# A two-layer decoder on one core: the first expert layer sorts its token-expert pairs into tiles and multiplies only the chosen ones

## What is computed

```python
TOP_K, NUM_EXPERTS = 4, 16          # H = 256, I = 224
logits = einsum('bsh,eh->bse', x, router_w) + expert_bias
top_w, top_idx = top_k(softmax(logits), TOP_K)
top_w = top_w / sum(top_w)
g = einsum('bsh,khe->bske', x, gate_proj)     # every expert, every token
u = einsum('bsh,khe->bske', x, up_proj)
out = einsum('bske,keh->bskh', silu(g) * u, down_proj)
sel = take_along_axis(out, top_idx)
y = sum(sel * top_w)                          # added to the residual stream
```

## Time and profile before

| | us |
|---|---|
| median of 3 runs | 4774.38 (4768.8 to 4774.94) |
| the profiled execution | 4788.41, of which span 4786.6 |
| set attention: its loads start / its first matmul | 707 / 714 |
| expert layer: router loads start / main loop starts / last addition to `x` ends | 808 / 831 / 1497 |

### The profile page before, as it was taken

The page is one execution under the profiler, slowest core; times in us unless marked ns, Lnnn a source line. Parts: engine busy times, 40 slices in busy tenths (PEclk is TensorE's granted clock), DMA queues, the critical chain, the costliest instruction groups (busy, mean ns, idle before and its releaser), DMA issues. The chain is left out here.

```text
span 4786.6 us, 58979 instructions
## 1 busy us (share of the span) xinstructions
PE 3923.9 (82%) x18543; PEld 2940.0 (61%) x18543; DVE 2799.6 (58%) x7765; ACT 1611.4 (34%) x3960; POOL 1349.6 (28%) x2074
## 2 busy tenths in 40 slices
PE   6999976999997799999999999983999999960230
PEld 4666654555555578888888888872556565640230
DVE  4666654222222788888888888844666666653123
ACT  2444431111111455545455554521444444420000
POOL 0000000000000365455555455540111111116447
PEclk9999986999997999999999999996999999985665
DMA  1000000000000011111111111111000000011240
GB/s 65 0 0 0 0 8 24 12 12 23 12 12 18 20 37 23 41 38 24 36 23 40 35 29 36 24 18 51 1 0 0 0 0 0 0 64 58 60 143 13
DMA packets 198749, 119.39 MB, mean 25 GB/s; under 512 B 122312, under 2 KB 187654, under 8 KB 197520
## 3 DMA queue, kind: packets, MB, share of 16 engines
q1 hardware_dynamic: 181472, 102.85, 8.3%
q0 software_dynamic: 12288, 9.55, 0.7%
q10 hardware_dynamic: 4800, 4.72, 0.3%
HBM read 102.09 MB, written 38.93 MB: 29 GB/s over the span
## 5 line engine op out<-in xcount | busy, mean ns | idle before, releaser
L1630 DVE SCALAR_TENSOR_TENSOR dl_y<-ps,dl_taps,dl_y 128x255 f32<-128x255 f32 (+2 forms) x1536 | 653.0, 474 | 131.4 <-ACT dl_y L1526 127.3
L1361 PE MATMUL ps<-xnT,dl_wkqv 128*128 128x256 f32 x2048 | 543.4, 391 | 33.9 <-DVE dl_lp L1673 26.4
L923 PE MATMUL ps<-xnT,moe_wgu 128*112 x1024 | 447.3, 595 | 5.2 <-DVE moe_ex L963 5.2
L1361 PEld LDWEIGHTS ps<-xnT,dl_wkqv 128*128 128x128 f32 x2048 | 367.9, 193 | 84.0 <-issue 39.2
L923 PEld LDWEIGHTS ps<-xnT,moe_wgu 128*112 128x112 f32 x1024 | 181.9, 178 | 251.3 <-issue 249.3
L362 POOL TENSOR_TENSOR at_rs<-at_ss,mhalf 128x15 f32<-128x15 f32 x32 | 125.5, 3921 | 745.9 <-DVE at_ss L549 745.9
L183 POOL TENSOR_TENSOR ln_rstd<-ln_ve,mhalf 128x4 f32<-128x4 f32 x24 | 24.2, 1010 | 1084.0 <-DVE ln_ve L169 1084.0
L1284 POOL TENSOR_TENSOR dl_rn<-dl_n,mhalf 128x4 f32<-128x4 f32 x128 | 173.7, 1357 | 548.2 <-DVE dl_n L1646 548.2
L448 PE MATMUL ps<-at_shared,at_v 128*128 128x256 f32 (+2 forms) x1280 | 315.9, 380 | 4.6
L989 DVE TENSOR_TENSOR moe_hT<-moe_sg,ps 112x1024 f32<-112x1024 f32 x64 | 78.2, 1221 | 372.6 <-ACT moe_sg L947 372.6
L1526 ACT ACTIVATE dl_y<-ps,dl_taps 128x256 f32<-128x256 f32 x512 | 260.2, 560 | 95.4 <-PE ps L1361 95.4
(11 more groups left out here) (278 smaller groups left out, 8195.3 us busy)
## 6 DMA issues: line engine op xcount, KB each, us to landing
dl_grow<-decay_rows SPq DMA_DIRECT2D x128, 128.0 KB, 3.0
sp_wgu<-in_w1gu SPq DMA_DIRECT2D x12, 768.0 KB, 10.2
dl_wkqv<-in_w1kqv SPq DMA_DIRECT2D x16, 512.0 KB, 4.7
delta_diag<-dl_lp SPq DMA_DIRECT2D x512, 8.0 KB, 1.5
dl_diag<-delta_diag_tt SPq DMA_DIRECT2D x512, 8.0 KB, 1.7
moe_wgu<-in_w0gu SPq DMA_DIRECT2D x16, 448.0 KB, 3.7
slot_rows<-sp_zero SPq DMA_DIRECT2D x4, 1152.0 KB, 8.1
sp_wd<-in_w1d SPq DMA_DIRECT2D x12, 384.0 KB, 11.5
```

The costliest lines, as they stand in the source:

```text
L923: last = nc.tensor.matmul(k.ps[h][0:IC, m, :], wgu[q][h][:, c, m * IC:(m + 1) * IC], k.xnT[:, c, ds(g * (GT * P), GT * P)], start=c == 0, ...
L1361: last = nc.tensor.matmul(bank(h, m // 2, (m % 2) * S, (m % 2 + 1) * S), wkqv[h][:, c, m * P:(m + 1) * P], k.xnT[:, c, u.seq * S:(u.seq + ...
L1630: last = nc.vector.scalar_tensor_tensor(y[h][:, m, back:S], bank(h, m // 2, (m % 2) * S, (m % 2 + 1) * S - back), taps[h][:, m, KC - 1 - b ...
```

## The change

The layer is rewritten as `routed_experts`. What it does, in order:

- All 16 experts' weights are loaded at once into SBUF by a new `ExpertWeights`, 32 transfers (16 of 448 KB and 16 of 224 KB) that SP issues before `set_attention`.
- `layernorm` leaves its rows in `rows`, beside which DVE writes the 16 routing weights of each token. SP stores these 2,048 rows of 272 values in HBM (`xtab`) and `k.x` in HBM (`acc`).
- The pairs are counted and sorted: DVE makes running counts per expert, PE adds them over the partitions (three bf16 matmuls), and DVE works out each pair's slot in a list in which each expert's section is rounded up to a multiple of 128. For each of the 16 token tiles DVE writes 4 `lanes` and 4 `tiles` operands, and PE multiplies them into a [128, 79] table of row numbers, `index`. Unused slots point at rows of zeros.
- A loop over 79 tiles, written out without hardware loops. For tile i: POOL gathers 128 rows of `xtab` by indirect DMA (`fetch`), PE transposes them (`turn_x`), DVE copies them to SBUF (`keep_x`), PE makes gate and up with the rows as the loaded operand and 448 columns of weights moving, read at a register's expert number (`up`), ACT and DVE make the hidden values (`silu`, `gate`), PE transposes (`turn_h`), ACT copies (`keep_h`), PE makes the down product (`down`), ACT scales it by the pair's weight (`weigh`), and POOL adds the 128 rows to `acc` by an accumulating indirect DMA (`add`).
- At the end SP loads `acc` back into `k.x`.

The diff, without the semaphore and buffer declarations, the counting arithmetic and the old loop's removed streams:

```diff
+class ExpertWeights:
+            def _(sp):
+                for e in range(E0):
+                    sp.dma_start(self.gu[:, e, :].rearrange("p (c n) -> p c n", c=DC),
+                                 k.ins["w0gu"][e].rearrange("(c p) n -> p c n", p=P)).then_inc(self.loaded, 16)
+                    sp.dma_start(self.d[:, e, :].rearrange("p (c n) -> p c n", c=2),
+                                 k.ins["w0d"][e].rearrange("(c p) n -> p c n", p=IC)).then_inc(self.loaded, 16)
-def experts(k):
+def routed_experts(k, weights):
+    TILES = (T * TOPK0 + E0 * (P - 1)) // P
+    W = D + E0
+    ROWS = T + P
+    RX, RH, RY = 4, 2, 3
...
+        layernorm(k, rows[:, :, 0:D])
...
             def _(sp):
 ...
+                sp.dma_start(acc[0:T].rearrange("(t p) d -> p t d", p=P), k.x[:, :, :]).then_inc(stored, 16)
+                sp.wait_ge(zeroed, 1)
+                sp.dma_start(acc[T:ROWS], zero[:, 0:D]).then_inc(stored, 16)
+                sp.dma_start(xtab[T:ROWS], zero[:, :]).then_inc(stored, 16)
+                sp.wait_ge(weighed, 1)
+                sp.dma_start(xtab[0:T].rearrange("(t p) d -> p t d", p=P), rows[:, :, :]).then_inc(stored, 16)
+                sp.wait_ge(added, 16 * TILES)
+                for b in range(B):
+                    sp.dma_start(k.x[:, TB * b:TB * b + TB, :], 
+                                 acc[S * b:S * b + S].rearrange("(t p) d -> p t d", p=P)).then_inc(back, 16)
+                sp.wait_ge(back, 16 * B)
...
+            def _(pool):
+                def fetch(i):
+                    if i >= RX:
+                        pool.wait_ge(turned, i - RX + 1)
+                        pool.wait_ge(taken, i - RX + 1)
+                    nc.gpsimd.indirect_dma_start(
+                        out=xs[i % RX][:, :], out_offset=None, in_=xtab,
+                        in_offset=bass.IndirectOffsetOnAxis(index[:, i:i + 1], axis=0),
+                        bounds_check=ROWS - 1, oob_is_err=True).then_inc(fetched[i % RX], 16)
+                def add(i):
+                    pool.wait_ge(y_ready, i + 1)
+                    if i:
+                        pool.wait_ge(added, 16 * i)
+                    nc.gpsimd.indirect_dma_start(
+                        out=acc, out_offset=bass.IndirectOffsetOnAxis(index[:, i:i + 1], axis=0),
+                        in_=y[i % RY][:, :], in_offset=None, bounds_check=ROWS - 1, oob_is_err=True,
+                        compute_op=ALU.add).then_inc(added, 16)
+                pool.wait_ge(index_ready, 1)
+                pool.wait_ge(stored, 64)
+                for i in range(TILES + 3):
+                    if i < TILES:
+                        fetch(i)
+                    if i >= 3:
+                        add(i - 3)
...
+                def turn_x(i):
+                    pe.wait_ge(fetched[i % RX], 16 * (i // RX + 1))
...
+                turn_x(0)
+                for i in range(TILES + 2):
+                    if i < TILES:
+                        up(i)
+                    if 0 <= i - 1 < TILES:
+                        turn_h(i - 1)
+                    if i + 1 < TILES:
+                        turn_x(i + 1)
+                    if i >= 2:
+                        down(i - 2)
...
+                def weigh(i):
+                    act.wait_ge(down_ready, i + 1)
+                    act.wait_ge(taken, i + 1)
+                    if i >= RY:
+                        act.wait_ge(added, 16 * (i - RY + 1))
+                    nc.scalar.activation(y[i % RY][:, :], down_ps(i), ACT.Copy, scale=wcol[:, i:i + 1]).then_inc(y_ready, 1)
+                for i in range(TILES + 2):
+                    if 0 <= i - 1 < TILES:
+                        keep_h(i - 1)
+                    if i < TILES:
+                        silu(i)
+                    if i >= 2:
+                        weigh(i - 2)
...
+                for i in range(NT):
+                    if i >= 4:
+                        dve.wait_ge(placed, i - 3)
+                    for j in range(TOPK0):
+                        nc.vector.tensor_scalar(lanes[i % 4][:, j, :], iota[:, :], lo[:, i, j:j + 1], None, ALU.is_equal)
+                    for j in range(TOPK0):
+                        last = nc.vector.tensor_scalar(tiles[i % 4][:, j, :], iota[:, 0:TILES], hi[:, i, j:j + 1],
+                                                       ident_row[:, i:i + 1], ALU.is_equal, ALU.mult)
+                    last.then_inc(tiles_made, 1)
...
+                keep_x(0)
+                for i in range(TILES):
+                    take_weight(i)
+                    if i + 1 < TILES:
+                        keep_x(i + 1)
+                    gate(i)
...
-        with k.own_semaphores(""):
+        with ExitStack() as st, k.own_semaphores("_m"):
+            weights = ExpertWeights(k, st)
             set_attention(k)
-        layernorm(k)
-        with k.own_semaphores(""):
-            experts(k)
+            routed_experts(k, weights)
```

More of the change, by code:

```diff
@@ L871, in experts @@
         ex, tot, rtot = sb("ex", [P, NT, TOPK0]), sb("tot", [P, NT]), sb("rtot", [P, NT])
[L872 to L884, removed]
+        eq = sb("eq", [P, NT, TOPK0, E0])
@@ new lines, in routed_experts @@
+        part = sb("part", [P, NT, TOPK0, E0])
+        m = sb("m", [P, NT, E0], BF16)
+        PAD = NT // 2
+        scan = [sb(f"scan{i}", [P, PAD + NT, E0], BF16) for i in range(5)]
+        ends = [sb(f"ends{i}", [P, PAD + E0]) for i in range(5)]
+        base = sb("base", [P, E0])
+        table = sb("table", [P, NT, E0])
+        slot, hi, lo = sb("slot", [P, NT, TOPK0]), sb("hi", [P, NT, TOPK0]), sb("lo", [P, NT, TOPK0])
+        ident_row = sb("ident_row", [P, NT])
+        lanes = [sb(f"lanes{i}", [P, TOPK0, P]) for i in range(4)]
@@ new lines, in routed_experts @@
+        tiles = [sb(f"tiles{i}", [P, TOPK0, TILES]) for i in range(4)]
+        pad_row = sb("pad_row", [P, TILES])
+        index = sb("index", [P, TILES], U32)
+        over = sb("over", [P, TILES, E0])
+        owner = sb("owner", [P, TILES])
+        pick = sb("pick", [P, TILES, E0])
+        ids = sb("ids", [P, TILES], I32)
+        xs = [sb(f"xs{q}", [P, W]) for q in range(RX)]
+        picked = [sb(f"picked{q}", [P, E0]) for q in range(2)]
+        wcol = sb("wcol", [P, TILES])
+        xT = [sb(f"xT{q}", [P, DC, P]) for q in range(2)]
@@ L891, in _ @@
                 sp.dma_start(bias[:, :], ins["w0rb"].partition_broadcast(P)).then_inc(loaded, 16)
[L892 to L901, removed]
+                sp.dma_start(iota[:, :], ins["c_iota"]).then_inc(loaded, 16)
@@ new lines, in _ @@
+                sp.wait_ge(weighed, 1)
[5 more added lines that the diff above has]
+                sp.wait_ge(back, 16 * B)
+            @block.gpsimd
+            def _(pool):
+                nc.gpsimd.memset(zero[:, :], 0.0).then_inc(zeroed, 1)
+                for i in range(5):
+                    nc.gpsimd.memset(scan[i][:, 0:PAD, :], 0.0)
+                    last = nc.gpsimd.memset(ends[i][:, 0:PAD], 0.0)
+                last.then_inc(zeroed, 1)
+                def fetch(i):
[21 more added lines that the diff above has]
+                        add(i - 3)
@@ L910, in _ @@
                 last.then_inc(routed, 1)
[L912 to L935, removed]
@@ new lines, in _ @@
+                for i in range(NT):
+                    pe.wait_ge(tiles_made, i + 1)
+                    for j in range(TOPK0):
+                        last = nc.tensor.matmul(k.ps[0][:, 1, 0:TILES], lanes[i % 4][:, j, :], tiles[i % 4][:, j, :],
+                                                start=i == 0 and j == 0, stop=i == NT - 1 and j == TOPK0 - 1)
+                    last.then_inc(placed, 1)
+                pe.wait_ge(weights.loaded, 16 * 2 * E0)
+                pe.wait_ge(ids_ready, 1)
@@ new lines, in _ @@
+                expert = {}
+                def turn_x(i):
+                    pe.wait_ge(fetched[i % RX], 16 * (i // RX + 1))
+                    if i >= 2:
+                        pe.wait_ge(x_kept, i - 1)
+                    else:
+                        pe.wait_ge(index_ready, 1)
+                    for c in range(DC):
+                        last = nc.tensor.transpose(x_ps(i)[:, c * P:(c + 1) * P], xs[i % RX][:, c * P:(c + 1) * P], k.ident[:, :])
+                    last.then_inc(turned, 1)
@@ new lines, in up @@
+                def up(i):
+                    expert[i] = pe.value_load(ids[0:1, i:i + 1], min_val=0, max_val=E0 - 1)
+                    pe.wait_ge(x_kept, i + 1)
+                    if i >= 2:
+                        pe.wait_ge(act_ready, i - 1)
+                    for c in range(DC):
+                        last = nc.tensor.matmul(up_ps(i), xT[i % 2][:, c, :],
+                                                weights.gu[:, ds(expert[i], 1), c * 2 * I0:(c + 1) * 2 * I0].rearrange("p e n -> p (e n)"),
+                                                start=c == 0, stop=c == DC - 1)
+                    last.then_inc(up_ready, 1)
```

(24 more changed lines are left out.)

144 lines of the change are left out of this document (122 added, 22 removed).

## The result

The changed kernel takes 4872.49 us (median of 4 runs, 4865.3 to 4876.43), the kernel before 4774.66 (4 runs beside them): a ratio of 1.0202, 95% interval 1.0184 to 1.0221. That is 98 us slower, where 4880 was forecast.

What follows compares the result with a forecast made beforehand. TensorE's multiplications bound the old loop (666 us); in the new one a round trip per tile. 75 periods of 8.4 us, loop ends, sorting and 34 us of earlier delay made 105 us more: 4880 us, range 4745 to 5070.

Steps and rivals of the forecast that it cites:

- TensorE's work falls, and it isn't the bound: Tile loop: 221 us of PE work replace 666, but PE doesn't stay the bound, so 445 us don't go.
- The order decides; each tile pays a round trip: Tile loop: gather i must land before the add ahead of gather i+1 can be issued; four buffers don't help.
- The period: Per tile: gather 3.05, turn_x and down 2.3, weigh 0.55, POOL's start 1.2, add until next gather 1.3; sum 8.4 us.
- the signs of being wrong: Profile after: POOL released by added, gathers several tiles ahead, a pair every 6.7 us, or accumulating calls holding POOL over 1 us.
- The gather: Tile loop, from its start on POOL to the reader's start: 3.05 us, bounds 2.15 and 4.5.
- The clock: PE's turn_x and down until ACT starts: mostly half clock, so 2.3 us, between 2.5 at half and 1.5 at full.
- Weights ahead of set attention: 11.0 MB queued on SP at 317 GB/s, 35 us: set attention starts about 32 us later, bounds 12 and 45.
- Sorting: Before the tile loop, counting, slots, index operands and storing xtab: first gather at about 888 instead of 831, 57 us.
- Ends of the loop: First tile until add(0) about 20 us; after 75 periods, last tiles and landing 19, loading back into k.x 11.
- the quick round trip: Rival: gather lands in 2.15 us and PE keeps full clock, period 6.7, kernel 4752 us; chance 0.13.
- The bound by adds: Rival: each add waits for the one before to land, deciding from 8.4 us; period 13 gives 5224 us; chance 0.17.
- the third rival: The change does what it says: gathers run ahead in the tile loop; period 4.5 gives 4587 us; chance 0.05.

Runs made afterwards that it cites:

- filled_wait_2: The changed kernel with three more 256-column matmuls between turn_h and turn_x, while PE would wait for the gather: 4848.1 us, ratio 1.0132.
- adds_two_later: The changed kernel with add(i-5) instead of add(i-3) issued behind fetch(i) on POOL: 4614.0 us, ratio 0.9635.

## Why the prediction was right

- *TensorE's work falls, and it isn't the bound.* Right: PE's share in the loop is 60% with less work, and the time went up.
- *The order decides; each tile pays a round trip.* Right, and shown three ways: opened on POOL (0.9635), opened on PE (0.9776), and not opened by buffers (1.0193).
- *The period.* 8.4 forecast, 8.31 to 8.34 measured. That it came so close is luck: the accumulating call holds POOL 1.59 us, so its term is 1.89 and not 1.3 (inside the bound of 2.6). The other four terms were together 0.67 too large, over half of it because POOL starts 0.82 after its release, not 1.2, and this made up for the 0.59. A call longer than 1 us stood among the signs of being wrong, and this one came in part. The 1.29 in the earlier trace rows was of a scatter beside which DVE was busy; whether that made it longer wasn't tried.
- *The gather.* 2.95 against 3.05. The row with full calls was the one to go by. (The upper bound of this term adds up to 4.6, not 4.5; nothing hangs on it.) The Trainium skill's rule for a transfer started by GpSimd ("DMA: Bandwidth & Descriptors", Anatomy of one DMA) gives 2.3 us for these bytes, as an estimate. The trace doesn't agree with it: 2.95 us, and no less than 2.83 in the 57 tiles.
- *The clock.* "Mostly half" was right for the stretch that it prices. From `turn_x` until ACT starts it was 2.43 or 2.44 us in 39 of the 57 tiles and 1.36 to 1.39 in 8. The 0.72 is the mean of the whole loop. That the clock prices this stretch is shown by `filled_wait_2`.
- *Weights ahead of set attention.* 32 us forecast, 40 measured, and the rate was the term that was mis-sized. While the weights moved, the DMA engines were busy all the time at 266 GB/s, not 317 (columns as in the earlier trace rows):

```profile
707.00:740.00 33.00, 0.00 (x0) 0.00 (x0) 0.00 (x0) 0.16 (x1) 0.00 (x0) 0.50 1.02 266
```

At 266 GB/s the 11.0 MB take 41 us and not 35. SP was held back with them: it issued set attention's first load 32.9 us later than before, took 7.1 us for the six (739.84 to 746.94) and not 3.3 (706.90 to 710.16), and the first matmul came 7.1 us behind the last issue and not 4.0.

- *Sorting.* 57 forecast, 49.4 measured. A `tensor_scalar` takes 0.21 us in its row, not 0.26: 128 of them in 27.3 us, where 33 were forecast.
- *Ends of the loop.* 18.2 for 20, and 34.1 for 38 (the last period of 8.4, then 19 and 11).

The layer was forecast 105 us longer and is 92.7: the weights cost 6 us more than forecast, and sorting, loop and ends together 18 less. The rivals: the quick round trip needed 2.15 for the gather, which it never showed (2.83 at the least). The bound by adds lay at 4.4 to 4.7, not above 8.4; it came only when the circle was opened. And the third rival's loop is `adds_two_later`: what the change brings with another order. Its period was put at 4.5 and is 4.70.

## What to carry to other kernels

Where two queues each issue a request for a later tile and a result of an earlier one in fixed order, write down for one tile who must be done before whom, across all queues. If the wait for the newest request stands ahead of the oldest result on one queue, and the oldest result ahead of the next request on the other, more buffers don't help, and each tile costs the sum of the latencies. Here another order on either one of the queues was worth 200 to 270 us.

## What the runs showed of the hardware

- An indirect call that accumulates holds POOL for 1.59 us, one that writes 1.03, for the same 128 rows of 1 KB; adds that wait for each other follow at 4.4 to 4.9 us, writes that do at 3.3.
- A transfer of 128 gathered rows of 1,088 bytes lands 2.9 us after its call starts (2.8 to 3.1 over the run), and whether the transfer just ahead of it accumulates or only writes changes that by 0.05.
- Matmuls of no use, put where TensorE waited for a transfer, made the kernel 33 us faster, with the granted clock of the loop up from 0.72 to 0.88.
- 32 transfers of 448 and 224 KB on one queue moved 266 GB/s with the DMA engines busy all the time, and six small loads behind them landed 7.5 to 10.4 us after their issue.
